# A selective scan beside a top-2 mixture of experts: the expert tiles spread over the scan, nine for eight scan units

## The reference

```python
# attn: tokens of each batch are sorted by the nearest of 8 cluster means, then a selective scan runs over them
xs = take_along_axis(x, sort_idx)                      # (B, 2048, 256), u = xs transposed
x_dbl = einsum('bdl,cd->bcl', u, x_proj_weight)        # 32 delta ranks, 16 B rows, 16 C rows
delta = softplus(dts @ dt_w + dt_b)
def step(h, (u_t, d_t, b_t, c_t)):                     # h: (B, 256 channels, 16 states)
    h = exp(d_t[..., None] * A) * h + (d_t * u_t)[..., None] * b_t[:, None, :]
    return h, einsum('bdn,bn->bd', h, c_t)
out = take_along_axis(y, inv_idx)                      # back to token order
# ffn: 8 experts, hidden 512, the top 2 of them for each token
h = silu(xt @ w1[e]) * (xt @ w3[e]);  y = h @ w2[e];  out = sum over the 2 experts of probs * y
```

## Time and profile before

| | |
|---|---|
| median of 3 runs | 810.21 us (808.32 to 811.06) |
| the profiled execution | 817.38 us, span from first to last instruction 815.3 us |
| busy share of the span | PE 81%, PEld 52%, DVE 84%, ACT 53%, POOL 73% |
| granted TensorE clock, mean | 0.913 |
| DVE's first product of the scan, last scan unit's end | 170.85 us, 747.06 us |

### The profile page before, as it was taken

The page is one execution under the profiler, slowest core; times in us unless marked ns, Lnnn a source line. Parts: engine busy times, 40 slices in busy tenths (PEclk is TensorE's granted clock), DMA queues, the critical chain, the costliest instruction groups (busy, mean ns, idle before and its releaser), DMA issues. The chain is left out here.

```text
span 815.3 us, 15751 instructions
## 1 busy us (share of the span) xinstructions
PE 663.9 (81%) x4538; PEld 422.7 (52%) x4539; DVE 682.9 (84%) x882; ACT 431.0 (53%) x926; POOL 597.3 (73%) x372
## 2 busy tenths in 40 slices
PE   3734889788998798989998898999889798989870
PEld 2523745245655465556655565565556555655550
DVE  5769777579999999999999999999999999997110
ACT  1324656465655556656655575566557554653320
POOL 3728800038788898988989898888989898889532
PEclk9866955599999989999999998999999998999995
DMA  7972659979944754674575466547645654662322
GB/s 228 371 259 91 180 206 297 321 221 241 210 102 103 144 118 87 146 150 94 115 163 111 89 149 138 105 90 164 139 90 125 134 127 90 142 142 35 49 27 26
DMA packets 76845, 118.63 MB, mean 146 GB/s; under 512 B 22456, under 2 KB 56848, under 8 KB 74512
## 3 DMA queue, kind: packets, MB, share of 16 engines
q1 hardware_dynamic: 54656, 90.95, 41.2%
q0 software_dynamic: 19824, 27.16, 19.4%
q10 hardware_dynamic: 2336, 0.15, 0.2%
...
## 5 line engine op out<-in xcount | busy, mean ns | idle before, releaser
L534 POOL TENSOR_TENSOR ring<-ring,bc 128x1024 f32<-128x1024 f32 (+2 forms) x128 | 308.0, 2424 | 38.9 <-DVE state L1047 38.0
L1044 DVE TENSOR_TENSOR_SCAN ring<-ring,state,pb 128x512 f32<-128x512 f32 x256 | 313.8, 1267 | 4.6
L654 ACT ACTIVATE ring<-late,aneg 128x512 f32<-128x512 f32 x256 | 164.2, 721 | 12.0 <-DMA late<-dd_d 9.1
L1035 DVE TENSOR_TENSOR pb<-fb,bc 128x1024 f32<-128x1024 f32 x128 | 157.3, 1229 | 3.0
L1284 PE MATMUL py<-w2x,pool 128*128 x568 | 141.6, 395 | 0.5 <-ACT pool L726 0.3
L1267 PE MATMUL fa<-w,pool 128*128 x284 | 137.7, 608 | 3.9 <-issue 2.8
L506 POOL DMA_INDIRECT out_dram<-pool,meta x71 | 112.9, 1590 | 29.8 <-issue 15.7
L1267 PE MATMUL fb<-w,pool 128*128 x284 | 134.3, 596 | 0.0
L486 POOL DMA_INDIRECT pool<-xn_d,meta x71 | 71.3, 1004 | 81.3 <-DVE ids L1001 33.5
L1284 PEld LDWEIGHTS py<-w2x,pool 128*128 128x128 f32 x568 | 107.7, 200 | 13.6 <-issue 1.0
L1267 PEld LDWEIGHTS fb<-w,pool 128*128 128x128 f32 x284 | 54.5, 192 | 68.9 <-issue 68.9
...
## 6 DMA issues: line engine op xcount, KB each, us to landing
late<-dd_d SPq DMA_DIRECT2D x256, 128.0 KB
...
w<-in_L_ffn_w_dram SPq DMA_DIRECT2D x16, 512.0 KB, 8.6
ring<-in_L_attn_x_dram SPq DMA_DIRECT2D x8, 512.0 KB, 4.3
out_dram<-ring SPq DMA_DIRECT2D x8, 512.0 KB, 7.7
xn_d<-w2x SPq DMA_DIRECT2D x8, 512.0 KB, 8.6
dd_d<-pool SPq DMA_DIRECT2D x8, 512.0 KB
dd_d<-ring SPq DMA_DIRECT2D x8, 512.0 KB, 5.1
```

Of the source, the lines that this page charges most:

```text
L534: ins = po.tensor_tensor(r, r, c_rows, ALU.mult)
L654: ins = ac.activation(ring[:, g % RING, n, :], dd[:, g % 2, 0, :], ACT.Exp, scale=aneg[:, NH * g + n:NH * g + n + 1])
L1035: ve.tensor_tensor(pb[:, :].rearrange("p (n c) -> p n c", n=2), pd[:, :].rearrange("p (o c) -> p o c", o=1).to_broadcast([P, 2, CH]), b_ro ...
L1044: ve.tensor_tensor_scan(r, r, pb[:, CH * m:CH * m + CH], state[:, NH * g + n:NH * g + n + 1], ALU.mult, ALU.add).then_inc(S["scan_done"], 1)
```

## The change

Time is counted in beats. A unit has six beats on DVE: product, scan, scan, product, scan, scan (`BEATS`). Tile j has its silu at beat 6 + (48j+1)//9, so that nine tiles stand beside eight units, the first of them at the start of unit 1, and all 71 end within the 64 units. `unit_beside(j)` is the unit that begins between tile j-1 and tile j; it is none for one tile in nine. All engines place their steps by these beats, and all loops are written out. With it come: six gather buffers instead of four, three `ye` buffers instead of two, two output buffers `ya` used in turn instead of `hand_over`'s copy, one load of nine index columns instead of nine loads (`load_meta`; from chunk 1 on it waits on SP for an add to land), a last half multiply on DVE, the four scan adds of the last chunk behind the last tile's add under one wait, and on ACT `exps` and `put_du` of unit 0 before the first tile. In the first chunk SP issues the w3 and w2 loads of a unit without the wait for a turned tile. The core of the diff:

```diff
-SPI = G
-SCAN_STEPS = (3, 3, 7, 7)
-REST_SCAN_STEPS = (1, 2, 3, 4)
-assert len(SCAN_STEPS) == TPC and SCAN_STEPS[-1] == SPI - 1
-REST = range(SPI * NCH + 1, FT)
+UNITS = NCH * G
+BEATS = 6
+SCAN_UNITS = {3: (0, 1), 7: (2, 3)}
+XR, XT, YE = 6, 4, 3
+BLOCK = G + 1
...
+        def beat_of(j):
+            return BEATS + (BEATS * G * j + 1) // BLOCK
+
+        beats = {beat_of(j): j for j in range(FT)}
+
+        def tile_at(beat):
+
+            return beats.get(beat)
+
+        def unit_beside(j):
+
+            u = beat_of(j) // BEATS
+            return u if j == 0 or beat_of(j - 1) // BEATS < u else None
+
+        ADD_LATER = BEATS
...
+            for u in range(UNITS):
+                c, g = u // G, u % G
+                if u >= 2:
+                    load_dd(u)
+                if c == 0 and g + EARLY < E:
+                    load_up(g + EARLY, w3, w3_in)
+                    load_down(g + EARLY)
+                if g == 3 and c + 1 < NCH:
+                    if c:
+                        sp.wait_ge(S["hc_done"], G * c)
+                    sp.wait_ge(S["bc_in"], 128 * (c + 1))
+                if 3 <= g < 3 + P // DG and c + 1 < NCH:
+                    load_bc(c + 1, g - 3)
+                if g == 3 and 0 < c < NCH - 1:
+                    sp.wait_ge(S["meta_in"], 16 * (c + 1))
+                    sp.wait_ge(S["added"], landed_expert(BLOCK * c - 1))
+                    load_meta(c + 1)
...
+            def add_expert(j):
+
+                po.wait_ge(S["ye_done"], j + 2)
+                po.wait_ge(S["added"], landed_expert(j) - 16)
+                po.indirect_dma_start(out[:, :], bass.IndirectOffsetOnAxis(ap=meta.bitcast(U32)[:, j % (2 * BLOCK), 0:1], axis=0),
+                                      ye[j % YE], None, compute_op=ALU.add).then_inc(S["added"], 16)
+
+            def add_scan(c, n, after):
+
+                po.wait_ge(S["ya_done"], G * (c + 1))
+                po.wait_ge(S["added"], after)
+                po.indirect_dma_start(out[:, :], bass.IndirectOffsetOnAxis(ap=ids[:, TPC * c + n:TPC * c + n + 1], axis=0),
+                                      ya[c % 2][:, n, :], None, compute_op=ALU.add).then_inc(S["added"], 16)
+
...
+            for beat in range(BEATS, beat_of(FT - 1) + ADD_LATER + 1):
+                u = beat // BEATS - 1
+                c, g = u // G, u % G
+                if beat % BEATS == 0:
+                    scans = SCAN_UNITS.get(g, ()) if c else ()
+                    split = 1 if scans else NH // 2
+                    po.wait_ge(S["h_ready"], u + 1)
+                    done = multiply(u, slice(0, split))
+                    for n in scans:
+                        add_scan(c - 1, n, landed_scan(c - 1, scans[0]) - 16)
+                    if u == UNITS - 1:
+                        if split < NH // 2:
+                            done = multiply(u, slice(split, NH // 2))
+                        done.then_inc(S["hc_done"], 1)
+                j = tile_at(beat - ADD_LATER)
+                if j is not None:
+                    if j + XR < FT:
+                        gather(j + XR)
+                    add_expert(j)
+                if beat % BEATS == BEATS // 2 and u < UNITS - 1:
+                    multiply(u, slice(split, NH)).then_inc(S["hc_done"], 1)
+            for n in range(TPC):
+                add_scan(NCH - 1, n, landed_expert(FT - 1))
+            po.wait_ge(S["added"], landed_expert(FT - 1) + 16 * TPC)
...
+            exps(0)
+            put_du(0)
+            evac_xt(0)
+            exps(1)
+            tanh(0)
+            for beat in range(BEATS // 2, beat_of(FT - 1) + 2):
+                if beat % BEATS == BEATS - 2 and beat // BEATS + 1 < UNITS:
+                    put_du(beat // BEATS + 1)
+                if beat == BEATS:
+                    evac_xt(1)
+                    exps(2)
+                j = tile_at(beat - 1)
+                if j is not None and j + 1 < FT:
+                    tanh(j + 1)
+                j = tile_at(beat - 2)
+                if j is not None and j + 1 < FT:
+                    evac_ht(j)
+                    u = unit_beside(j + 1)
+                    if u is not None and u >= 3:
+                        take_y(u - 3)
+                    if u is not None and u >= 2:
+                        take_sum(u - 2)
+                    if j + 2 < FT:
+                        evac_xt(j + 2)
+                    if u is not None and u + 1 < UNITS:
+                        exps(u + 1)
+                j = tile_at(beat - BEATS + 1)
+                if j is not None:
+                    evac_y(j)
             evac_ht(FT - 1)
-            evac_y(FT - 1, (FT - 1) % 2, (FT - 1) % SPI, turn_of(FT - 3))
+            take_y(UNITS - 3)
+            take_sum(UNITS - 2)
+            evac_y(FT - 1)
+            take_y(UNITS - 2)
+            take_sum(UNITS - 1)
+            take_y(UNITS - 1)
...
+            for u in range(UNITS):
+                for beat in range(BEATS):
+                    j = tile_at(BEATS * u + beat)
+                    if j is not None:
+                        silu(j)
+                    if beat % 3 == 0:
+                        product(u, beat // 3)
+                    else:
+                        scan(u, 2 * (beat // 3) + beat % 3 - 1)
+                keep_states(u)
+                if u + 1 == G * CPB:
+                    ve.wait_ge(S["h_ready"], u + 1)
+                    ve.memset(state[:, :], 0.0).then_inc(S["state_cleared"], 1)
+                    ve.wait_ge(S["state_cleared"], 1)
+            last_u = UNITS - 1
+            ve.wait_ge(S["h_ready"], UNITS)
+            r = ring[:, last_u % RING, NH // 2:NH, :].rearrange("p n c -> p (n c)")
+            ve.tensor_tensor(r, r, bc[:, last_u // G % 2, 1, NH // 2:NH, :].rearrange("p n c -> p (n c)"),
+                             ALU.mult).then_inc(S["hc_last"], 1)
...
+            for j in range(1, FT):
+                u = unit_beside(j)
+                if j == G + 1:
+                    pe.wait_ge(S["w3_in"], 16 * E)
+                    pe.wait_ge(S["w2_in"], 16 * E)
+                up(j, e_up)
                 e_next = expert_of(j + 1) if j + 1 < FT else None
-                turn_h(j - 1, (j - 1) % 2)
+                turn_h(j - 1)
                 pe.wait_ge(S["ye_done"], j)
-                if j - REST[0] < 3:
-                    fold_units(NCH, j - REST[0])
+                if u is not None and u >= 3:
+                    turn_y(u - 3)
+                if u is not None and u >= 2:
+                    fold_states(u - 2)
+                pe.wait_ge(S["ht_done"], j)
                 if j + 1 < FT:
-                    after_scan = j - REST[0] >= 3
-                    if after_scan:
-                        pe.wait_ge(S["ya_done"], G * NCH)
-                    else:
-                        pe.wait_ge(S["ht_done"], j)
-                    turn_x((j + 1) % 4, 16 * ((j + 1) // 4 + 1), pd if after_scan else pt)
-                if j - REST[0] < 3:
-                    units_read(NCH, j - REST[0])
-                down(j - 1, e_down, (j - 1) % 4)
+                    turn_x(j + 1)
+                if u is not None and u >= 3:
+                    pe.wait_ge(S["ya_done"], u - 2)
+                if u is not None and u >= 2:
+                    pe.wait_ge(S["y1_done"], u - 1)
+                down(j - 1, e_down)
                 e_down, e_up = e_up, e_next
-            pe.wait_ge(S["ht_done"], FT - 1)
-            turn_h(FT - 1, (FT - 1) % 2)
+            turn_h(FT - 1)
```

480 lines of the change are left out of this document (150 added, 330 removed).

## The result

The changed kernel took 879.41 us (median of 4, 876.41 to 880.68), the kernel before 810.54 (4 runs, 808.32 to 811.06): ratio 1.0849, 95% interval 1.0813 to 1.0885, so slower. The forecast was 840 us, with a range from 790 to 866. The sign was right, the size was not. The profiled execution has a span of 876.5 us.

What follows compares the result with a forecast made beforehand. DVE bounds the kernel up to 747 us, then the adds; after the change, waits through POOL and ACT slow DVE. 166 + 94 + 6 x 84 + 83.3 = 847 us of span, 7 off gives 840, range 790 to 866.

Steps and rivals of the forecast that it cites:

- the last step: From profiled span to median: the same 7 us taken off as before the change, 847 to 840 us.
- The ends: Start and finish: first product near 162 us, chunk 0's head 94 us, last units to the span's end 83.3 us.
- POOL's and ACT's orders: Adds between POOL's multiplies and put_du behind take_sum and exps on ACT delay DVE's products, 60 to 75 us in all.
- the walk of one chunk: Step-by-step timing from the end of unit 9: a chunk takes 84 us where DVE's work is 72.5.
- The first term: On POOL, unit 3's scan pair waits about 1.4 us for the landing of the add before.
- The second: At a chunk's head, POOL without arrears: unit 15 ends at 55.8 and unit 17 at 84.0 us.
- the 7.5: On PE, from a fold's start to the end of the next `up`: 7.5 us.
- A: POOL's occupancy alone binds, 76.3 us a chunk: span 801, median 794 us, faster; chance 0.14.
- D: As forecast, but PE's clock falls at each wait, 3.4 us once a chunk and at the end: 864 us; chance 0.12.
- C: DVE remains the bound throughout: span 768, median 761 us; chance 0.06.
- B: put_du harmless, but silu(8c+10) waits for PE behind the late fold: 80 us a chunk, median 816; chance 0.08.
- E: Written-out code makes an engine wait for instructions: +5 us at most, about 845 us; chance 0.02.

Runs made afterwards that it cites:

- undoing both: Changed kernel with put_du ahead of take_sum on ACT and both multiplies of a unit together on POOL: ratio 1.0177 to the kernel before.
- again: The changed kernel, unaltered, measured once more on the chip of a later batch: ratio 1.0854 to the kernel before.
- no bc loads: Changed kernel without loading the B and C rows of chunks 2 to 7 (stale rows used): one execution of 863.15 us.
- PE busy, no bc loads: Changed kernel with 24 extra PE matmuls ahead of the folds of units 3 and 7, without bc loads of chunks 2 to 7: ratio 1.0820.
- the best version: Changed kernel, put_du ahead of take_sum on ACT, a unit's multiplies together, in units 3 and 7 ahead of the scan-add pair: ratio 1.0080 to the kernel before.

## Why the prediction failed in size

**From span to median.** The median lies 39.4 us above the forecast, the span 29.5 above its 847. The other 9.9 are the last step: I took 7 us off the span, since the profiled execution before was 7.2 us above its median. The profiled execution of the changed kernel, 879.56, is at its median and 3.1 above its span.

**The ends.** Nearly right: the first product came at 156.31 (162 forecast), but unit 9 ended at 263.94 against 260.0: units 6 and 8 of chunk 0 took 14.1 and 14.8 us. POOL waits there too, 4.81 us for the landing of an add in front of the one at 205.25, though chunk 0 has no scan adds. In the change's second profile unit 6 of chunk 0 took 8.9 us and unit 9 ended at 260.36. From the last unit's end to the end of the span it was 876.5 - 847.07 = 29.4 (27.4 forecast, 68.2 before).

**POOL's and ACT's orders.** Right in kind, and shown: undoing both gives back 54 of 69 us. DVE's waits were 115.2 us in 30 where I forecast 60 to 75, because there are three places in a chunk with long ones (units 6, 8 and 9) and not two. PE's fold waits over 4 us twice a chunk, not once.

**The step that failed** is the walk of one chunk, in two of its terms. The table has the walk beside the traces of four runs, as means of six chunks in us from the end of unit 9; for a fold the walk's figure is the end of the second multiply, for which it waits.

| | walk | change | again | no bc loads | PE busy, no bc loads |
|---|---|---|---|---|---|
| fold of unit 11 starts | 29.0 | 31.6 | 30.8 | 29.2 | 31.2 (POOL done at 28.9) |
| fold of unit 12 starts | 39.9 | 42.6 | 42.4 | 40.1 | 40.4 |
| DVE ends unit 14 | 44.5 | 48.8 | 49.2 | 45.5 | 47.1 |
| DVE ends unit 15 | 55.8 | 58.4 | 58.1 | 56.4 | 56.1 |
| fold of unit 14 starts | 55.5 | 60.7 | 60.5 | 58.8 | 58.6 |
| fold of unit 15 starts | 69.4 | 73.6 | 73.4 | 71.7 | 72.1 |
| DVE ends unit 17 | 84.0 | 88.35 | 88.1 | 86.4 | 85.8 |

The first term is the wait of unit 11's pair for the landing: 1.4 in the sum, 3.7 to 5.05 measured in the six chunks that load bc rows, 1.67 in chunk 7, which loads none. With it POOL is late by 2.6 us at the fold of unit 11, and so is DVE at the end of unit 15. Without the loads unit 15 ends at 56.4, within 0.6 of the walk, and the chunk is 1.9 us shorter. That is shown, by one execution and by the run with PE busy.

The second is the head of the chunk. The walk has 28.2 us from the end of unit 15 to that of unit 17, with POOL at unit 15 as soon as DVE is done ("if POOL has no arrears"); the traces of all four have 29.7 to 30.0. POOL had arrears, since its second multiplies stand in a circle with PE's folds and ACT's scaled y: from the fold of unit 12 to that of unit 14 it is 18.1 us where the walk has 15.6, and the walk put the adds' waits for ACT at nothing. With the two multiplies of a unit together, which breaks the circle, it is 16.3. That this is what makes the head 1.8 us longer is read from the timelines; no run shows it alone. So the 4.35 us are 2.6 up to unit 15 and 1.8 behind it.

PE's slow stretch, for which the walk had nothing, is a small part of it: 5.9 instead of 5.5 us from the fold of unit 15 to `put_du`, and 0.7 to 1 us by the runs.

The walk has two more errors, which matter little for the chunk. DVE ends unit 14 at 44.5 in it as if nothing stood there, though `put_du` of unit 14 stands behind the fold of unit 11; by my own prices (29.0, 7.5 to the end of `up`, tanh and `put_du` 0.6 each) it comes at 37.7 and DVE asks for it at 35.6. But 2.1 us there change nothing at unit 15, which waits for its own `put_du` behind the fold of unit 12. And the 7.5 is the price to the end of the whole `up`, while tanh needs `fa` alone, at 4.03 + 1.88 = 5.9 us with PE at full clock.

**The rivals.** A (POOL's occupancy alone) is refuted: with the same POOL work in another order the chunk goes from 88.35 to 79.7. D (the clock) was right as a mechanism; its price was 3.4 us a chunk and measured about 1. C did not come: DVE is not the bound. B's wait was not there in the change, where DVE's silus waited for PE next to nothing (1.2 us in four places from 260 to 760 us); it came with `put_du` out of the way (40.4 us for tanh, chunk 85.95 where B had 80). No run tested E. What is not explained is the remaining 79.7 against DVE's 72.5 in the best version. POOL, PE and DVE are each busy 67 to 71 of 80 us there, and every edit that moved an add or a `put_du` moved the wait to another fold; which of them would have to give is open.
